# A token mixer with its sums, its lent bank and its conversion at other places of the step

## What is computed

```python
h = _L0_tok_ref(x)                                # token mixer: x is (128, 96, 512)
h = h + _L0_attn_ref(_layernorm(h, axis=-1), ...)
h = h + _L0_ffn_ref(_layernorm(h, axis=-1), ...)
h = h + _L1_attn_ref(_layernorm(h, axis=-1), ...)
h = h + _L1_ffn_ref(_layernorm(h, axis=-1), ...)

def _L0_tok_ref(qkv):                             # ch = 32, T = 512
    q, k, v = jnp.split(qkv, 3, axis=1)
    scale = 1.0 / np.sqrt(np.sqrt(ch))
    weight = jnp.einsum('bct,bcs->bts', q * scale, k * scale)
    weight = jax.nn.softmax(weight.astype(jnp.float32), axis=-1).astype(weight.dtype)
    return jnp.einsum('bts,bcs->bct', weight, v)
```

## Time and profile before

| | |
|---|---|
| median of 3 runs | 2335.91 us (2333.1 to 2338.05) |
| the profiled execution, its own time | 2331.95 us |
| its span | 2330.2 us |
| mixer: first exponential, last exponential | 27.4 us, 531.5 us |
| busy over the span: TensorE, VectorE, ScalarE, GpSimd | 94%, 72%, 65%, 54% |
| granted TensorE clock over the span | 0.99 of full speed |

### The profile page before, as it was taken

How to read it: one execution, slowest core, us unless ns; L and a number is a source line. 1 busy time by engine, 2 the same in 40 slices (tenths; PEclk the granted TensorE clock), 3 DMA queues, 4 the chain that set the end, 5 groups by cost and what they waited for, 6 DMA issues and landing times. The chain is left out here.

```text
span 2330.2 us, 42739 instructions
## 1 busy us (share of the span) xinstructions
PE 2189.6 (94%) x13828; PEld 1074.8 (46%) x13828; DVE 1677.4 (72%) x2922; ACT 1520.1 (65%) x2430; POOL 1267.9 (54%) x1141
## 2 busy tenths in 40 slices
PE   6899999987999998899999999999998999999997
PEld 1222222224666665444444444666664444444443
DVE  7777777775788988656667633666666788788775
ACT  4566666666688787446565424677665777777775
POOL 4566667667777778223234301444454566666654
PEclk9999999999999999999999999999999999999999
DMA  5444445441244221312223212222221011111111
GB/s 145 134 134 138 129 136 138 127 125 60 89 130 132 70 68 65 101 48 80 77 91 97 69 50 69 79 80 81 81 82 41 23 51 50 41 50 42 43 36 64
DMA packets 144050, 195.00 MB, mean 84 GB/s; under 512 B 30469, under 2 KB 73957, under 8 KB 143898
## 3 DMA queue, kind: packets, MB, share of 16 engines
q1 hardware_dynamic: 111642, 154.52, 21.8%
q10 hardware_dynamic: 32256, 38.54, 5.7%
HBM read 125.10 MB, written 42.21 MB: 72 GB/s over the span
## 5 line engine op out<-in xcount | busy, mean ns | idle before, releaser
L2293 PE MATMUL f_bank<-f_xs,gu 128*128 128x512 f16 x1408 | 417.0, 379 | 1.6 <-ACT f_firstg L2119 1.1
L371 DVE TENSOR_REDUCE tm_negmax<-tm_s 128x1 f32<-128x512 f32 x512 | 325.5, 682 | 90.7 <-PE tm_s L426 88.4
L321 ACT ACTIVATE tm_prob<-tm_s 128x1024 f32<-128x1024 f32 x256 | 258.6, 1025 | 192.7 <-PE tm_s L446 192.7
L2321 PE MATMUL f_bank<-dn,f_ghi 128*128 128x512 f16 x704 | 265.5, 379 | 1.9 <-DVE f_glo L2228 1.9
L274 POOL TENSOR_TENSOR tm_added<-tm_prob 128x1024 f32<-128x1024 f32 x96 | 224.6, 2354 | 33.8 <-ACT tm_prob L321 33.4
L2083 POOL TENSOR_TENSOR f_firstg<-f_firstg,f_secondg 128x512 f32<-128x512 f32 x88 | 152.4, 1731 | 152.7 <-DVE f_secondg L2212 152.7
L426 PE MATMUL tm_s<-tm_qk 96*128 96x512 f16 x512 | 200.8, 395 | 31.9 <-DVE tm_negmax L371 17.8
L446 PE MATMUL tm_s<-tm_qk 98*128 98x512 f16 x512 | 196.2, 386 | 32.2 <-ACT tm_prob L321 27.3
L2293 PEld LDWEIGHTS f_bank<-f_xs,gu 128*128 128x128 f16 x1408 | 135.9, 98 | 162.8 <-ACT f_firstg L2119 1.5
L2083 POOL TENSOR_TENSOR f_firstu<-f_firstu,f_secondu 128x512 f32<-128x512 f32 x88 | 123.9, 1408 | 64.3 <-DVE f_secondu L2212 64.2
L1048 PE MATMUL a_bankB<-a_wo,a_yThi 128*128 128x512 f16 x512 | 157.1, 389 | 0.0
(11 more groups left out here) (197 smaller groups left out, 5792.5 us busy)
## 6 DMA issues: line engine op xcount, KB each, us to landing
tm_qk<-tm_xs SPq DMA_DIRECT2D x384, 64.0 KB, 2.3
tm_xqk<-in_qk ACTq DMA_DIRECT2D x32, 512.0 KB, 4.7
...
```

Source lines behind the costliest of these rows:

```text
L321: nc.scalar.activation(prob[b][:, 2 * h:2 * h + 2, :], s2[:, i % 2, :, :], ACT.Exp, scale=SCALE).then_inc(exp_done, 1)
L371: nc.vector.tensor_reduce(negmax[u][:, m:m + 1], s1[:, BANK[p], :], AX.X, ALU.max, negate=True).then_inc(s1_read, 1)
L2293: last = nc.tensor.matmul(bank_of(m, i)[:, :], (gate, up)[which][:, j, m * P:(m + 1) * P], xs[g % 2][:, x, j, :], start=x == 0, stop=x == 1)
L2321: last = nc.tensor.matmul(pz[i][:, :], gparts[x][:, (MT * g + m) % RING, i * P:(i + 1) * P], down[w][:, m, :], start=m == 0 and c % 3 == 0 ...
```

## The change

On TensorE the two ones calls move from places 5 and 7 to places 7 and 10, `BANK` is another table, and bank 2 is lent from behind place 4 to place 12 (uses 6 and 15) where it was from behind place 2 to place 10 (uses 4 and 13). On ScalarE the conversion of x moves from behind exponential 4 to behind exponential 7, the values' copy from behind exponential 2 to behind 3, the sums' copy with its DMA issue from behind 3 to behind 4, and the store from behind 5 (of tile n - 2) to behind 1 (of tile n - 3). On GpSimd the low part of x comes second in a step, for tile n + 2, and `normalise` last. VectorE takes the reciprocal of a tile three places later, and SyncE's three transfers for it move. At the end of the mixer the same moves are written into the interleaving.

```diff
     BANKS = 3
     LEAD = 17
     E = B * T // P
-    BANK = (1, 2, 0, 1, 2, 0, 1, 0, 1, 0, 1, 0, 1, 2, 0, 1, 2, 0)
-    SUMS_BANK, FIRST_BEHIND_SUMS = 2, 13
+    BANK = (2, 0, 1, 2, 0, 1, 2, 0, 1, 0, 1, 0, 1, 0, 1, 2, 0, 1)
+    SUMS_BANK, LAST_BEFORE_SUMS, FIRST_BEHIND_SUMS = 2, 6, 15
     ident = sb("tm_ident", [P, P], F32)
     xqk = [sb(f"tm_xqk{i}", [P, 2, T], F32) for i in range(2)]
     xs = [sb(f"tm_xs{i}", [P, 4, T], F16) for i in range(2)]
...
 
     MAXIMA_AT = {9: 0, 1: 1}
     VALUES_AT = {14: (0, 0), 0: (1, 1), 2: (1, 2), 4: (1, 3)}
-    SUMS_AT = {5: 0, 7: 1}
+    SUMS_AT = {7: 0, 10: 1}
     BEFORE = [max(q for q in range(p - USES, p) if BANK[q % USES] == BANK[p]) for p in range(USES)]
 
     def unit(i):
...
         def step(k, u):
             n = 2 * k + u
             stack(n + 1, 1 - u, 2)
+            maxima(n, u, 1)
+            inverses(n - 2, u, k - 1)
+            stack(n + 1, 1 - u, 3)
             inverse_rows(n - 2, u, k - 1)
-            maxima(n, u, 1)
-            stack(n + 1, 1 - u, 3)
             stack(n + 2, u, 0)
             maxima(n + 1, 1 - u, 0)
             stack(n + 2, u, 1)
-            inverses(n - 1, 1 - u, k + u - 1)
         return step, store
 
     def rows_ready(sp, t):
...
         def step(k, u):
             n = 2 * k + u
             add(n - 1, 2)
+            x_lo(n + 2, u)
+            add(n, 0)
+            add(n, 1)
             if not isinstance(n, int) or n < TILES:
                 normalise(n - 2, u, k - 1)
-            add(n, 0)
-            add(n, 1)
-            x_lo(n + 3, 1 - u)
         return step, normalise
 
     def scalar(act):
...
             n = 2 * k + u
             for i in range(8):
                 exps(n, i)
+                if i == 1:
+                    store(n - 3, 1 - u)
                 if i == 2:
-                    copy_values(n - 1, 1 - u, k + u - 1)
                     load_values(n + 1, 1 - u)
                 if i == 3:
+                    copy_values(n - 1, 1 - u, k + u - 1)
+                if i == 4:
                     copy_sums(n - 1, 1 - u)
                     denominators(n - 1, 1 - u)
-                if i == 4:
-                    x_hi(n + 3, 1 - u, k + 1 + u)
                 if i == 5:
                     load(n + 4, u)
-                    store(n - 2, u)
-        return step, copy_values, copy_sums, denominators
+                if i == 7:
+                    x_hi(n + 3, 1 - u, k + 1 + u)
+        return step, store, copy_values, copy_sums, denominators
 
     def vector(dve):
         for u in range(2):
...
                 if pair is not None:
                     maxima_parts(n + 1 - pair, pair)
                 maxes(n + ahead, (u + ahead) % 2, m)
+                if g == 1:
+                    inverse_sums(n - 2, u, k - 1)
                 if g == 2:
                     add_last(n - 1)
-                if g == 14:
-                    inverse_sums(n - 1, 1 - u, k + u - 1)
         return step, inverse_sums, add_last
 
     def tensor(pe):
...
                         wait(pe, s1_read, use(t + 1, 16) + 1)
                         wait(pe, sums_out, t)
                     else:
-                        wait(pe, s1_read, use(t + 2, 4) + 1)
+                        wait(pe, s1_read, use(t + 2, LAST_BEFORE_SUMS) + 1)
                 out = sums_bank(t)
                 for b in range(B):
                     last = nc.tensor.matmul(out[C * b:C * (b + 1), :], ones[:, :], added[b][:, j, :],
...
         prepare(2)
         prepare(3)
         prepare(BEGIN)
-        run(step, -5, -4)
-        run(mix, 31, 31)
-        run(step, -3, -3)
-        run(mix, 32, 32)
+        run(step, -5, -3)
+        run(mix, 31, 32)
         run(step, -2, -2)
         prepare(WO)
         run(step, -1, 2)
...
 
     @block.scalar
     def _(act):
-        mix, copy_values, copy_sums, denominators = mixer.scalar(act)
+        mix, store, copy_values, copy_sums, denominators = mixer.scalar(act)
         prepare, step = att.scalar(act)
         run(mix, -4, -1)
         for i in range(WO):
...
         run(step, -5, -4)
         run(mix, 31, 31)
         run(step, -3, -3)
+        store(29, 1)
         copy_values(31, 1, 15)
         run(step, -2, -2)
         copy_sums(31, 1)
...
         run(step, -3, -3)
         add_last(31)
         run(step, -2, 0)
-        inverse_sums(31, 1, 15)
+        inverse_sums(30, 0, 15)
         statistics, normalised, low, _, _ = ternary.vector(dve)
         for n in range(1, 34):
             step(n // 2, n % 2, statistics, normalised, low)
+            if n == 1:
+                inverse_sums(31, 1, 15)
             beside_vector(dve, n)
 
     @block.tensor
```

## The result

The changed kernel takes 2353.16 us (median of 4 runs, 2352.4 to 2356.62), the kernel before in the same comparison 2334.72: ratio 1.0081, interval 1.0065 to 1.0097. It is slower by 0.8%, 4.9 us over the predicted 2348.3 and inside the range. The profiled spans are 2350.6 and 2330.2, 20.4 apart. The helpers' lines have moved by 2 (L446 is L448 now, L434 is L436, L479 is L481, L397 is L399, L371 is L373); ScalarE's and GpSimd's lines are the same.

What follows compares the result with a forecast made beforehand. No engine was full, so queue order was taken to set the pace. +0.35 us a tile over steps 1 to 28 (+9.8), with start and end terms, gave +12.4 on the 2335.91 median: 2348.3 us, range 2336 to 2359.

Steps and rivals of the forecast that it cites:

- A: TensorE from the maxima's turn at place 1 to place 9: 8.06 to 7.35 us, one ones call (1.09) less, 0.38 new wait.
- The new wait at place 7: In the stretch from place 1 to 9: max matmuls of places 5 and 7 share bank 0, 0.30 us, VectorE's delay up to 0.16 more.
- B: TensorE from the turn at place 9 to the score matmul of place 14: 4.39 us before, +1.06 forecast.
- The issue's hold: On ScalarE the sums' DMA issue holds exponential 5 behind the copy: 0.19 + 0.57 + 0.10 = 0.86 us.
- C: TensorE from place 14's score matmul to the next turn at place 1: stays 3.35 us, conversion hidden with 0.37 to spare.
- The rival of the late store: In the loop, the store lands late and delays `copy_values`; at a landing of 6.4 us, some 2370; chance 7%.
- the second ring: Not in the prediction: loop from ones call through GpSimd's four instructions, VectorE's held addition, reductions and TensorE, 16.15 us a tile.
- the first rival: In the loop, the DMA issue does not hold exponential 5: tile -0.47 us, the whole 2324; chance 9%.
- Start and step 0: Before the loop: second load of x may slow the first, +0.5 us; step 0 loses the conversion's wait, gets bank wait, -0.7.
- Steps 29 and 30: Mixer's steps without a conversion: the stretch from place 9 to 14 goes from 3.37 to 5.25 us; +1.2 each, +2.3 together.
- Step 31: Mixer's last step: the sums' copy moves behind exponential 4 and holds exponential 5 instead, +0.5 us as an estimate.
- Handover: Mixer to attention: VectorE's 5.56 us wait for tile 30's sums goes, but TensorE didn't wait for it; 0 (-1 to +1).

Runs made afterwards that it cites:

- the clean tiles: Changed kernel with GpSimd's multiplication ahead of its additions, VectorE's addition at place 1; tiles where that addition got its turn: DMA issue behind exponential 5 15.32 us, ahead 16.12.
- the run with GpSimd's edit alone: Changed kernel with the attention's preparation and steps -5 and -4 ahead of two low weight parts in GpSimd's order round step 31: 2354.05 us, ratio 1.0095.
- those with SyncE's edit: Changed kernel with the mixer's calls 32 and 33 one attention step later in SyncE's order: 2350.09 us; with GpSimd's order round step 31 changed too: 2348.04 us.

## Why the prediction came out, and where it didn't

- **A, 7.35 forecast, 7.31 measured.** The ones' part is confirmed by putting them back (8.04 without the held addition, against 8.06). The new wait at place 7 is 0.17 and not 0.30 to 0.46, and its cause is VectorE behind its addition.
- **B, 5.45 forecast, 5.50 measured.** Copy, issue, exponential stand as worked out from the earlier trace rows, each within 0.1 us. The issue's hold is 0.78 by moving it and 0.80 between the clean tiles.
- **C 3.35, conversion hidden.** It is: exponential 0 at 414.64 waits 0.33 for TensorE, the forecast cover was 0.37. `copy_values` runs right behind exponential 3 (404.45), not held by the store. The rival of the late store is out.
- **What the tile's sum left out** is the second ring. The prediction said of GpSimd that its additions "move about 3 us later in the tile, with `normalise` behind them", and went no further than "needed only at place 7". It didn't ask what VectorE's addition meets there. The forecast held because the ring has 16.15, too. That it isn't longer is luck: nothing in the prediction had bounded it. For the first rival (the issue doesn't hold exponential 5, 2324) the price was wrong: with the hold taken away the kernel took 2355.25. The lever that I named as deciding was not one by itself.
- **Start and step 0:** I had -0.2 and a growth of 0.35 a tile, which makes +1.2 at 107 us (place 1 of step 5); the distance there was 0.0. The 23 tiles from there to step 28 gave +8.1, as forecast. Step 28 gave -0.8 instead of +0.35, since in the kernel before TensorE waited 1.56 us there for the maxima's DMA (at 479.98), which I hadn't counted and the changed kernel doesn't have. Steps 29 and 30 gave +2.5 against +2.3. Together that is 2.1 less than forecast.
- **Step 31, +0.5 forecast, +3.8 measured.** The estimate counted the copy on ScalarE alone. It left out GpSimd's queue, where the mixer's later work stands ahead of the attention's deviation and of the third addition (taking one of them out brings in the other), and it left out the clock, about 1.6 of the 3.8. What the 2.2 us at full clock consist of stays open.
- **Handover, 0 (-1 to +1) forecast, +4.3 measured.** "TensorE didn't wait for that" was true of the sums of tile 30 and beside the point: I followed the reciprocal and not what is queued behind its DMAs on SyncE. Step 31 and the handover together are 8.1 - 0.5 = 7.6 us short. Of the 4.3, 0.4 arise while the granted clock is at half (557.8 to 561.2).
- **The clock, which had no term.** A further 1.3 arise between 630 and 648 us, where the changed kernel has half clock for 6.8 us (from 639.7) and the kernel before for 3.4 (from 622.6). The run with GpSimd's edit alone has none there and its distance falls by 1.5; those with SyncE's edit have 6.8 and gain 1.3 and 1.5. Another 1.2 arise between 930 and 1456 us, where the half clock comes as 6.8 + 3.4 + 3.4 us instead of 6.8 + 6.8; where it came as in the kernel before, in the run with GpSimd's edit alone, the distance grew by 0.15 only. With 1.6 in step 31 and 0.4 in the handover that is some 4.5 of the 20.4 us. The mean granted clocks, 0.988 and 0.990, say about the same: what they leave out of full speed is 28.2 us and 23.3 us.
- **Together.** Between the profiled executions 7.6 + 2.5 - 2.1 = 8.0 is what the 20.4 measured are above the 12.4 forecast. Between the medians the difference is 18.4, 6.0 above the forecast, and the kernel before came out 1.2 lower than the median that I had added to, so the time is 4.9 above the forecast one. That this lies inside the range is in part luck: two terms at the end of the mixer and the clock were missing, and the 2.1 too many elsewhere took some of it back.

**A version that beats both** came out of it: the kernel before with only the conversion moved (and `x_lo` with it), and VectorE's addition at place 3: 2313.2 us, 0.9913 of the kernel before.
